# Graph attention on one core: one gathered tile of 48 fetched row by row from SyncE and ScalarE instead of by GpSimd

## The reference

```python
def gat_conv(x, src, dst, W, att_src, att_dst, bias, n_nodes):
    h = (x @ W).reshape(n_nodes, Hh, Cc)
    a_src = (h * att_src).sum(-1)
    a_dst = (h * att_dst).sum(-1)
    alpha = leaky_relu(a_src[src] + a_dst[dst])
    m = jax.ops.segment_max(alpha, dst, num_segments=n_nodes)
    e = jnp.exp(alpha - m[dst])
    denom = jax.ops.segment_sum(e, dst, num_segments=n_nodes)
    w = e / jnp.clip(denom, 1e-16)[dst]
    out = jax.ops.segment_sum(w[:, :, None] * h[src], dst, num_segments=n_nodes)
    return out.reshape(n_nodes, Hh * Cc) + bias
...
    x = _layernorm(x + _L0_gnn_ref(x, edge_index, ...), axis=-1)   # two gat_conv layers, 4 heads
    x = _layernorm(x + _L1_gnn_ref(x, src, dst, ...), axis=-1)     # linear, then a layer with 8 heads
```

## Time and profile before

| | us |
|---|---|
| median of 3 runs | 9704.55 (9652.79 to 9725.02) |
| span of the profiled execution, first to last instruction | 6847.6 |
| median less span: lies outside the profiled instructions | 2857.0 |
| edge phases, first gather to last, three layers | 1967.3, 1978.3, 2003.8 |

### The profile page before, as it was taken

One profiled execution on the slowest core, in us unless ns is written; L12 is line 12 of the kernel. 1 busy time (PEld: TensorE's weight loads), 2 busy tenths in 40 slices (PEclk: granted clock), 3 DMA queues, 4 the chain that ended last, 5 costly groups with the idle time before them and its releaser, 6 DMA issues. The chain is left out here.

```text
span 6847.6 us, 108602 instructions
## 1 busy us (share of the span) xinstructions
PE 5239.0 (77%) x23932; PEld 3843.3 (56%) x23933; DVE 5132.5 (75%) x15279; ACT 2122.3 (31%) x3760; POOL 4922.7 (72%) x5329
## 2 busy tenths in 40 slices
PE   6787878787777678788787878777888888888860
PEld 4555655555555455555555555565656666666540
DVE  5777777777777677777777777777777777777779
ACT  3222222222223522222222222572222322322214
POOL 2777777777774677777777777577777777777757
PEclk8777777777778777777777777887777777777775
DMA  7444444444444554544454445464545555455534
GB/s 271 140 143 140 144 140 144 140 145 140 144 140 114 159 144 140 144 140 145 139 144 140 144 140 138 140 201 140 147 142 145 144 143 147 143 143 147 143 92 136
DMA packets 476120, 995.76 MB, mean 145 GB/s; under 512 B 143984, under 2 KB 283620, under 8 KB 475586
## 3 DMA queue, kind: packets, MB, share of 16 engines
q0 software_dynamic: 226928, 635.50, 34.0%
q1 hardware_dynamic: 192512, 305.60, 14.0%
q10 hardware_dynamic: 56402, 51.96, 2.2%
HBM read 921.47 MB, written 71.19 MB: 145 GB/s over the span
## 5 line engine op out<-in xcount | busy, mean ns | idle before, releaser
L1035 POOL DMA_INDIRECT e_rows<-table,e_loaded x4704 | 4479.9, 952 | 1566.6 <-issue 1409.8
L1108 PE MATMUL e_p_mm<-e_rows,e_onehot 128*128 128x264 f32 x9408 | 2488.1, 423 | 0.0
L1108 PEld LDWEIGHTS e_p_mm<-e_rows,e_onehot 128*128 128x128 f32 x9408 | 1928.5, 211 | 386.2 <-issue 20.4
L1230 DVE TENSOR_TENSOR e_rows<-e_rows,e_p_e 128x1024 f32<-128x1024 f32 x1176 | 1419.1, 1207 | 0.0
L1222 DVE TENSOR_TENSOR e_onehot<-e_col,e_p_iota 128x512 f32<-128x512 f32 (+1 forms) x1470 | 951.2, 647 | 303.8 <-issue 283.5
L1319 DVE TENSOR_TENSOR_SCAN e_fwd<-e_mask,e_p_one 64x128 f32<-64x128 bf16 (+1 forms) x294 | 121.8, 414 | 1033.8 <-PE e_p_one L1158 1032.1
L1101 PE MATMUL e_p_mm<-e_xmsg,e_onehot 128*128 128x264 f32 x1764 | 884.4, 674 | 0.0
L1081 ACT ACTIVATE e_rows<-e_gap 128x64 f32<-128x64 f32 (+1 forms) x294 | 80.6, 274 | 2434.3 <-DVE e_gap L1388 2434.3
L1166 PE MATMUL e_p_small<-ident,e_fwd 64*1 64x64 f32 (+1 forms) x588 | 106.2, 271 | 822.7 <-issue 811.0
L1063 ACT ACTIVATE e_onehotT<-e_onehotT,minus_pidx 128x2432 bf16<-128x2432 bf16 x294 | 681.6, 2318 | 43.1 <-DMA e_pass<-pass_rows 42.4
L1066 ACT ACTIVATE e_onehotT<-e_onehotT,one_col 128x2432 bf16<-128x2432 bf16 x294 | 682.7, 2322 | 9.6
(11 more groups left out here) (229 smaller groups left out, 6011.7 us busy)
## 6 DMA issues: line engine op xcount, KB each, us to landing
e_onehotT<-rel_rows SPq DMA_DIRECT2D x294, 608.0 KB
e_rows<-table,e_loaded POOLq DMA_INDIRECT x4704
n_looprow<-table SPq DMA_DIRECT2D x196, 128.0 KB, 2.6
table<-n_row ACTq DMA_DIRECT2D x98, 132.0 KB, 2.0
table<-n_rows_out SPq DMA_DIRECT2D x14, 910.0 KB, 10.9
table<-n_row ACTq DMA_DIRECT2D x98, 130.0 KB, 2.9
n_inputs<-in_x_turned SPq DMA_DIRECT2D x14, 896.0 KB, 11.0
e_mask<-mask_rows SPq DMA_DIRECT2D x196, 64.0 KB
```

What stands on the lines that cost most here:

```text
L1035: pool.indirect_dma_start(rows[k][:, g, 0:TW], None, table[L], bass.IndirectOffsetOnAxis(ap=idx[k][:, g:g + 1], axis=0)).then_inc(s_gat[k] ...
L1108: ins = nc.tensor.matmul(p_mm[:, bass.ds(region, MW)], onehot[:, g, :], rows[k][:, g, :], start=False, stop=True, skip_group_check=True)
L1230: return nc.vector.tensor_tensor(feats, feats, p_e[:, g4, :].unsqueeze(3).to_broadcast([P, 4, H, C]), ALU.mult)
```

## The change

The last tile (g = 15) of every window with k = 2 is no longer gathered by POOL. Its 128 rows are fetched one row to a DMA: 86 rows from SP's queue and 42 from ACT's, spread over three windows' bodies (30, 26 and 30 rows on SP, 14 a window on ACT), into a buffer of its own, `stage`. Each row is copied as two halves of 520 or 528 bytes; in `stage` one unused word lies between them. ACT copies `stage` into `rows[2][:, 15]` ahead of the window's `srcc`. Lists of node numbers come to one partition by small DMAs (one on SP, one on ACT, each three windows), and a TENSOR_LOAD takes them to registers ahead of each batch. The room for GpSimd's DMA descriptors is halved to 8192 bytes a partition (`dynamic_dma_scratch_size`).

```diff
+FETCH_SP, FETCH_ACT = (30, 26, 30), (14, 14, 14)
+FETCHED = sum(FETCH_SP)
...
+            HALF = TW // 2
+            stage = sbuf(ph, tag + "stage", [P, 2, HALF + 1], F32)
+            lists = sbuf(ph, tag + "lists", [33, P], I32)
+            list_sp, list_act = lists[0:1, 0:FETCHED], lists[32:33, FETCHED:P]
...
+            def fetch_rows(engine, names, first, s_part):
+                nodes = nc.values_load_multi_w_load_instructions(
+                    names, engines=[engine.engine], min_val=0, max_val=NODES_PAD - 1,
+                    skip_runtime_bounds_check_because="node numbers of edges")[1]
+                for p, node in enumerate(nodes):
+                    engine.dma_start(stage[first + p:first + p + 1, :, 0:HALF],
+                                     table[L][bass.ds(node, 1), :].rearrange("o (a c) -> o a c", a=2)).then_inc(s_part, 16)
...
-                    for g in range(G):
+                    for g in range(G - (k == BUFS - 1)):
...
 @block.sync
+                at_sp = (FETCH_SP[1] + FETCH_SP[2], 0, FETCH_SP[1])
+
+                def part_of_tile(w, k, turns):
+                    if k == 1:
+                        wait_apart(sp, s_copied, turns - 1)
+                        wait_apart(sp, s_list_sp, turns * 16)
+                    fetch_rows(sp, list_sp[:, at_sp[k]:at_sp[k] + FETCH_SP[k]], at_sp[k], s_part_sp[k])
+                def next_list(turns):
+                    group = turns - 1
+                    sp.dma_start(list_sp, t["fetch_rows"][bass.ds(group, 1), 0:FETCHED]).then_inc(s_list_sp, 16)
 
                 def body(w, k, turns, ago, first):
                     wait_apart(sp, st["cols"], ago(BUFS))
                     sp.dma_start(loaded[k][:], col_dram[:, bass.ds(w * COL_W, COL_W)]).then_inc(s_idx[k], 16)
+                    if not (isinstance(w, int) and w in (0, WINDOWS - 1)):
+                        part_of_tile(w, k, turns)
+                    if k == 0 and not (isinstance(w, int) and w > 0):
+                        next_list(turns)
                     wait_apart(sp, st["settled"], ago(BUFS))
...
 @block.scalar
+                def copy_tile(k, turns, ago):
+                    for j in range(BUFS):
+                        act.wait_ge(s_part_sp[j], turns * (16 * FETCH_SP[j]))
+                    act.wait_ge(s_part_act, turns * (16 * sum(FETCH_ACT)))
+                    wait(act, s_mm[G // 4 - 1], ago(BUFS))
+                    nc.scalar.copy(rows[k][:, G - 1, 0:TW].rearrange("p (a c) -> p a c", a=2), stage[:, :, 0:HALF]
+                                   ).then_inc(s_copied, 1)
+                    act.wait_ge(s_copied, turns)
+
                 def body(w, k, turns, ago, first):
                     now, past = ago(0), ago(1)
                     if first:
+                        next_list(0)
                         lookup_rows(k, turns, now)
-                    act.wait_ge(s_gat[k], turns * (16 * G))
+                        part_of_tile(BUFS - 1, 1)
+                    if k == BUFS - 1:
+                        copy_tile(k, turns, ago)
+                    act.wait_ge(s_gat[k], turns * (16 * (G - (k == BUFS - 1))))
...
                     if not (isinstance(w, int) and w == WINDOWS - 1):
                         lookup_rows((k + 1) % BUFS, count(act, turns + (k + 1) // BUFS), count(act, now + 1))
+                    if not (isinstance(w, int) and w >= WINDOWS // BUFS * BUFS):
+                        part_of_tile(k, count(act, turns + 1))
+                        if k == 1:
+                            next_list(turns)
                     act.wait_ge(st["gap"], now)
...
-    nc = bacc.Bacc("TRN2", target_bir_lowering=False, num_devices=1)
+    nc = bacc.Bacc("TRN2", target_bir_lowering=False, num_devices=1, dynamic_dma_scratch_size=8192)
```

More of the change, by code:

```diff
@@ L60 @@
 PASSES_AT, TABLES_AT, TURN_AT, FOLD_AT, BIAS_AT, LATER_AT = 42, 60, 76, 84, 90, 4
+FETCH_SP, FETCH_ACT = (30, 26, 30), (14, 14, 14)
+FETCHED = sum(FETCH_SP)
+assert FETCHED + sum(FETCH_ACT) == P
 BIG = 1e30
@@ L347, in _ @@
             def _(pool):
-                for x in [*per_layer, *s.values(), *s_node, *s_loop, *s_res, *s_row, *s_out, *s_rst]:
+                for x in [*per_layer, *per_fetch(), *s.values(), *s_node, *s_loop, *s_res, *s_row, *s_out, *s_rst]:
                     pool.sem_clear(x)
@@ L931, in build_program @@
     per_layer = [*s_idx, *s_ld, s_turn, s_done, s_step]
+    per_fetch = lambda: [*s_part_sp, s_part_act, s_list_sp, s_list_act, s_copied]
     s_clear = sem("e_clear")
@@ L935, in build_program @@
     s_apart = sem("e_apart")
+    s_part_sp = [sem(f"e_part_sp{k}") for k in range(BUFS)]
+    s_part_act, s_list_sp, s_list_act, s_copied = (sem(f"e_{n}") for n in ("part_act", "list_sp", "list_act", "copied"))
     def edge_phase(L):
@@ L1067, in lookup_rows, with next_list, part_of_tile @@
                                          ).then_inc(st["onehotT"], 1)
+                at_act = (FETCH_ACT[2], FETCH_ACT[2] + FETCH_ACT[0], 0)
+                def next_list(group):
+                    act.dma_start(list_act, t["fetch_rows"][bass.ds(group, 1), FETCHED:P]).then_inc(s_list_act, 16)
+                def part_of_tile(k, lists_in):
+                    if k == BUFS - 1:
+                        wait_apart(act, s_list_act, lists_in * 16)
+                    fetch_rows(act, list_act[:, at_act[k]:at_act[k] + FETCH_ACT[k]], FETCHED + at_act[k], s_part_act)
+                def copy_tile(k, turns, ago):
[6 more added lines that the diff above has]
+                    act.wait_ge(s_copied, turns)
                 def body(w, k, turns, ago, first):
@@ L1087, in _ @@
                 walk(act, body)
+                act.wait_ge(s_part_act, (WINDOWS // BUFS * sum(FETCH_ACT) + FETCH_ACT[2]) * 16)
+                act.wait_ge(s_list_act, (WINDOWS // BUFS + 1) * 16)
             @block.tensor
@@ L1449 @@
     edge_rows = edge_rows.reshape(SG, P, P + 2).transpose(1, 0, 2).reshape(P, SG * (P + 2))
+    fetch_rows = np.zeros((WINDOWS // BUFS + 1, P), src.dtype)
+    fetch_rows[:-1] = src_pad.reshape(WINDOWS, G, P)[BUFS - 1::BUFS, G - 1]
     def columns(a):
@@ L1465 @@
         "x_pad": x_pad, "x_turned": np.ascontiguousarray(x_turned), "edge_rows": np.ascontiguousarray(edge_rows), "edge_cols": np.ascontiguousarray(edge_cols),
-        "dst_rows": dst_rows, "tile_ends": np.concatenate([tile_first, tile_base, tile_last])[None],
+        "dst_rows": dst_rows, "fetch_rows": fetch_rows, "tile_ends": np.concatenate([tile_first, tile_base, tile_last])[None],
         "tile_base": np.ascontiguousarray(tile_base_rows.reshape(SG, P).T), "window_ends": window_ends,
```

## The result

| | before | after | ratio |
|---|---|---|---|
| first timing, where 9704.55 us was measured (4 runs each) | 9705.5 us | 13740.6 us (13727.8 to 13750.6) | 1.419, interval 1.416 to 1.422 |
| on another chip (7 and 4 runs of it) | 6847.95 us | 9716.17 us (9706.0 to 9723.2) | 1.419, interval 1.417 to 1.422 |
| forecast | 9704.55 us | 11,620 us (10,400 to 13,120) | 1.197 |

The kernel is slower, as forecast, but by twice as much, and the time lies outside the range. One thing has to be cleared first: the kernels run at two paces. Where the first timing was made they need 9705 and 13740 us; on four of the six other chips of the experiments 6848 and 9716 us. I call these the slow and the usual pace. The ratio is the same (by the medians alone 1.416 and 1.419).

What follows compares the result with a forecast made beforehand. POOL bounds the kernel; SP's 80.7 us turn (rows 67.1, old copies 9.4, loads 3.6, list 0.55) replaces it. The excess over three layers, 59.8 us times 32 turns, adds 1914 to 9704.55: 11,620 us, range 10,400 to 13,120.

Steps and rivals of the forecast that it cites:

- What bounds the kernel: In the edge phases: POOL's gathers bound the old kernel, 58.8 us a turn after; SP takes over with 80.7.
- The row's price: On SP's queue: 0.575 us of issue plus 0.20 around it, 0.78 us a row, 86 rows a turn.
- The price by the number of engines: SP's rows: two DMA engines serve one, so it costs no less than `mask`, 0.84 us; about 12,110 us in all.
- The register loads: On SP, ahead of each batch of rows: 1.2 us each, 3.6 us for the three in a turn.
- ScalarE's rows beside SyncE's: Both issuing queues: nothing in the sum; delay by a shared descriptor generator named under the much slower rival, 13,110 us, chance 0.16.
- The jump back: At the end of SP's loop: makes one of a turn's three windows of old copies 0.26 us longer.
- The ring: Halved descriptor room for POOL's gathers: costs zero; even 1411 us of longer gather waits would add nothing.
- ScalarE's pause and the copy out of `stage`: On ACT: 12.1 us of rows and load in an 8.09 us pause, and a 0.5 us copy; both hidden in 26.9 us windows.
- What lies around the span, 2857 us by it, I carry over unchanged: Whole kernel: median time 9704.55 us exceeds the profiled span 6847.6 by 2857 us, which stays the same after the change.
- 0.57 case: SP's rows at 0.57 to 0.65 us each; at 0.57 a turn is 62.6 us, 9880 us in all; chance 0.06.
- windows longer than SP's sum: Edge windows in the profile after: forecast 26 to 27 us; longer than SP's own sum would show the prediction wrong.
- as `passes`: Much slower rival, SP's rows at `passes`' price, 0.96 us each: 96.2 us a turn, 13,110 us in all; chance 0.16.

Runs made afterwards that it cites:

- Experiment 6: Changed kernel with all 128 rows copied in one piece into a `stage` without the gap: 6822.84 us, then 6824.43, 0.9965 of the kernel before.
- experiment 8: Changed kernel with SyncE's rows split 30, 28, 28, then 30, 25, 31, to move list starts: 13414.5 and 13678.33 us at the slow pace.
- experiment 2: Kernel before with only the descriptor room halved to 8192 bytes: 6844.59 us, 0.9985 of the kernel before.
- experiment 9: Kernel before unchanged, and changed kernel without ScalarE's 42 row copies a turn: 9732.26 and 13208.21 us at the slow pace; the latter 9406.47 at the usual.
- experiment 5: Changed kernel with each register list cut to its first number, used for all rows of the part, the 128 copies kept: 8187.98 us.
- experiment 7: Changed kernel with its two-piece rows split 68 on SyncE and 60 on ScalarE a turn: 7969.8 us.

## Why the prediction was wrong

- **What bounds the kernel: right.** SyncE takes GpSimd's place; its wait of 4919.4 us is gone, and `loaded` and `passes` are what GpSimd and ScalarE wait for.
- **The row's price: right.** 0.575 us forecast, 0.568 measured; with what stands around it 0.75 for 0.78. The issue's price, taken from the mask's copy less its partitions, held to 1.2%. No run varied the partitions or the pieces of a row by themselves, so this is one hit and not a tested rule. Experiment 6 agrees with the reason: the same bytes in one shape, and one piece, on both sides take 0.228 us, and the loss disappears. The price by the number of engines (a row no cheaper than `mask`, 12,110 us) doesn't hold: 0.568 us is under `mask`'s 0.61 to 0.64.
- **The register loads: mis-sized.** "I take 1.2, between 0.35 and 1.4; three make 3.6 us." They last 2.0, 2.3 and 6.3 us, 10.6 a turn. The bounds came from loads of 16 numbers at most, on other engines; 26 to 30 numbers lie beyond them. That is 7.0 x 96 = 672 us. The one of 6.3 us is slow because it starts at number 26 (experiment 8); I had not looked at the starts at all.
- **ScalarE's rows beside SyncE's: costed at nothing.** The prediction named a shared generator in half a sentence, among the rivals, and put nothing for it into the sum. They are worth 307 us (9716.17 less 9408.91), nearly all of it (296) for the second half of the rows.
- **The jump back: not counted beyond 0.26 us.** 2.6 us in the second layer, 31 times: 72 us.
- **The ring: right**, nothing (experiment 2). **ScalarE's pause and the copy out of `stage`: right as far as seen**; with ScalarE's rows alone nothing is lost (6820.63 us).
- **"What lies around the span, 2857 us by it, I carry over unchanged": wrong.** It is 1.8 us. The number was a difference of pace, and a pace multiplies: with the measured ratio of paces, 1.417, the forecast's own sum would have been (6847.6 + 1914) x 1.417 = 12,415 us. That one step made 796 us of the miss of 2121, the terms above about the rest.
- **The chances don't fit the range.** What the range leaves out (0.12, 0.06 and the 0.06 of the 0.57 case) is 0.24, not "a little under 0.2".

At the usual pace the sum stands so, in us: 1914 forecast, + 672 for the loads and 50 for the gaps behind them, + 307 for ScalarE's rows, + 72 for the jump, - 111 for rows that take 65.9 us a turn by the trace of SyncE alone and not 67.1, - 14 for the old copies = 2890; measured 9716.2 - 6848.0 = 2868. By turns: 80.7 forecast, 90.7 measured. The rest lies at the ends of a layer: its first turn grows by 3 us and not by 30, before SyncE's lateness reaches GpSimd, and the two windows behind the 32 turns grow by 20; over three layers that is 80 us less and 59 more. One of the prediction's own signs of being wrong, windows longer than SP's sum, is met. The rival "as `passes`" (13,110) comes near the measured 13,740 by its number only: the row's issue of 0.568 us refutes it.

**What stays open.** The slow pace goes with the chip: three showed it and four didn't. Each was met in one sitting, so a property of the chip and a passing state of it are not told apart. At the slow pace the engines that do much register work stall in steps of about 0.7 us: in the kernel before 621 of PE's register instructions last over 0.3 us and 78 of SyncE's, in the changed one 2365 of SyncE's and 1639 of ScalarE's. DVE has few (3 and 19), GpSimd none. Every kernel tried at both paces is stretched by 1.40 to 1.43. The fetching of instructions doesn't explain it by its amount: the kernel before moves the same 228 packets of them at both paces. That gathers cause the stalls is a coincidence in time that no run here changed; the DMA engines are busy in the same stretches (0.38 for 0.01), so their traffic is a rival. Why some chips do so is not known. In the first trace I had taken ScalarE's rows for the cause, since its bursts begin at the same moments as the gathers; experiment 9 refutes that.

## What to carry to other kernels

Before moving work to an idle queue, price one unit of it by what the sequencer does: a row in one piece on both sides, or in two with a gap on one side, is a factor of 2.5 in issue time here (0.228 and 0.568 us), and at 86 copies a turn that alone decided between 0.35% faster and 42% slower. Price register loads by their own size and start them at a multiple of four numbers: 30 cost 2.3 us so, 6.3 otherwise, where up to 16 had cost 0.8 on PE. When a variant drops one cost, count the instructions too: experiment 5 took out a register instruction ahead of each row besides the loads. And where the time on record and the profiled span differ by 40%, don't add a difference from one to the other: take ratios.

## What the runs showed of the hardware

- Row copies with one shape on both sides issue in 0.228 us, below every copy of the kernel before; with a gap in the destination's middle, 0.568.
- A load of registers on SyncE: 0.47 us for one number, 1.8 to 2.3 for 25 to 30 that start at a multiple of four numbers, 6.3 to 6.5 for 30 or 31 that don't. On ScalarE, 14 numbers: 1.4 us, or 3.2.
- A jump back over a loop body of 314 instructions took SyncE 2.6 to 3.2 us (kernel after, contiguous rows) in one layer and 0.21 to 0.26 in the others; the layer with the slow jump has some 150 packets more on the queue that fetches instructions (316 for 158 before, in the second layer). With 260 instructions (experiment 7) the first layer had it, 3.9 us; with 231 no layer did.
- At the slow pace, register instructions that take 0.03 to 0.04 us last up to 1.4 us and more, on PE, SyncE and ScalarE above all, while GpSimd's gathers (0.95 us) keep theirs and the busy times of PE, DVE and ScalarE stay within 3.2%.
- SyncE is held up a little when both issue long bursts of two-piece rows; ScalarE hardly is (at the usual pace 589 of SyncE's register instructions last over 0.3 us, 11 of ScalarE's). Both start at about full speed: ScalarE's 14 copies from 1517.3 to 1527.3 us stand beside 12 of SyncE's (first line). Then SyncE stalls in steps of 0.3 us and more, in register instructions too (second line): from 1526.1 to 1530.5 its four rows take 4.4 us for 3.0, and part of that lies behind ScalarE's last row, which ends at 1527.9.
```profile
L1030 SPq DMA_DIRECT2D e_stage<-table x12: 567/579/694, 1517.5 to 1526.1; - x12
...
L1030 SPq MOVE e_stage<-table x17: 19/29/321, 1528.9 to 1541.0; - x17
```
  With 7 rows a window on ScalarE, or with rows in one piece, SyncE has next to none, though one-piece rows bring nearly twice as many instructions in a time. So it goes with the pieces and not with the number of instructions; what it is, is open. The Trainium skill, "Perfetto Trace Analysis", section on the DMA instruction with hardware descriptors, says that sequencers share one descriptor generator, which is locked for the one at work. By that rule, two engines that both issue would wait for each other from their first copy on, and in copies alone. The trace shows 12 of SyncE's copies at a median of 0.579 us beside ScalarE's, for 0.568 alone, and stalls outside copies too.
